# Last feed-forward of a four-layer model: who multiplies gate and lifted columns, and one step of lag

## The reference, cut to what matters

```python
def fake_quant_nvfp4(x, global_scale):
    xb = x.reshape(sh[:-1] + (sh[-1] // BLOCK, BLOCK))
    amax = jnp.max(jnp.abs(xb), axis=-1, keepdims=True)
    sc = jnp.clip(amax / FP4_MAX * global_scale, 0.0, FP8_MAX)
    sc8 = sc.astype(jnp.float8_e4m3fn).astype(jnp.float32)
    dq = sc8 / global_scale
    a = jnp.clip(jnp.abs(xb) / safe_dq, 0.0, FP4_MAX)
    q = jnp.sign(xb) * _FP4_VALS[jnp.digitize(a, _FP4_MIDS)]
    return (q * dq).reshape(sh)
gate_out = nvfp4_linear(x, gate_w, s_in[0])
up_out = nvfp4_linear(x, up_w, s_in[0])
hidden = jax.nn.silu(gate_out) * up_out
return nvfp4_linear(hidden, down_w, s_in_down[0])
```

## Time and profile before

| what | us |
|---|---|
| median of three runs | 1085.5 |
| lowest and highest of them | 1084.51, 1087.7 |
| span of the profiled execution | 1084.4 |
| DVE busy in the span | 885.9 |
| POOL busy in the span | 523.1 |
| ACT busy in the span | 686.2 |

### The profile page before, as it was taken

How to read it: one execution, slowest core, us unless ns; L and a number is a source line. 1 busy time by engine, 2 the same in 40 slices (tenths; PEclk the granted TensorE clock), 3 DMA queues, 4 the chain that set the end, 5 groups by cost and what they waited for, 6 DMA issues and landing times.

```text
span 1084.4 us, 30129 instructions
## 1 busy us (share of the span) xinstructions
PE 898.7 (83%) x11539; PEld 707.4 (65%) x11557; DVE 885.9 (82%) x2296; ACT 686.2 (63%) x1794; POOL 523.1 (48%) x612
## 2 busy tenths in 40 slices
PE   8999999999999932999689999978899999434443
PEld 5888889978887721566457778834478888222222
DVE  6999888878999961567568889889978888899997
ACT  6888864377776610444447777866678888555553
POOL 6444412254367676223287787255553332355554
PEclk9999999999999966899889999988899999655665
DMA  8760000000000012365111111000000000000000
GB/s 214 186 241 2 3 2 2 1 2 3 3 24 27 27 46 76 114 187 175 51 33 32 26 31 29 6 1 2 1 2 2 2 3 3 1 10 16 15 15 24
DMA packets 60526, 44.42 MB, mean 41 GB/s; under 512 B 15196, under 2 KB 55781, under 8 KB 59366
## 3 DMA queue, kind: packets, MB, share of 16 engines
q1 hardware_dynamic: 55718, 34.09, 10.6%
q0 software_dynamic: 4096, 8.34, 2.7%
q10 hardware_dynamic: 576, 0.13, 0.1%
HBM read 23.73 MB, written 18.87 MB: 39 GB/s over the span
## 4 chain that ended last, share of the span: by engine, by line
PE 63%; DVE 21%; issue 6%; POOL 5%; ACT 2%; DVEq 2%; DMA 1%; POOLq 0%; another core or an unknown queue 0%; SPq 0%; ACTq 0%
PE ps L747 10%; PE ps L706 9%; PE ps L674 7%; PE ps L586 4%; PE ps L720 4%; PE ps L692 4%; POOL q_out L1232 3%; DVE rowmax L1879 3%; PE ps L782 3%; PE ps L791 3%; PE ps L783 3%; PE ps L640 2%; PE ps L655 2%; PE ps L653 2%; DVE sm L1885 2%
## 5 line engine op out<-in xcount | busy, mean ns | idle before, releaser
L1879 DVE TENSOR_REDUCE rowmax<-ps 128x16 f32<-128x1024 f32 x128 | 155.8, 1217 | 35.7 <-PE ps L674 34.4
L1885 DVE TENSOR_TENSOR sm<-ps,rowmax 128x512 f32<-128x512 f32 x256 | 164.9, 686 | 3.4
L1038 ACT ACTIVATE pr<-ps 128x512 f32<-128x512 f32 x256 | 138.9, 595 | 38.2 <-PE ps L747 36.0
L747 PE MATMUL ps<-cst,sm 128*128 128x128 f32 x1024 | 138.9, 277 | 13.3 <-DVE sm L1885 12.2
L706 PE MATMUL ps<-vbd,pr 128*64 128x18 f32 x4096 | 140.3, 211 | 0.5 <-ACT pr L1038 0.5
L706 PEld LDWEIGHTS ps<-vbd,pr 128*64 128x64 f32 x4096 | 134.2, 138 | 1.4 <-ACT pr L1038 1.3
L1320 POOL TENSOR_SCALAR xn<-x_sb,mv_all,rstd_all 128x128 f32<-128x128 f32 x122 | 98.2, 805 | 71.7 <-PE ps L640 65.7
L747 PEld LDWEIGHTS ps<-cst,sm 128*128 128x128 f32 x1024 | 112.8, 141 | 26.3 <-issue 19.5
L938 ACT ACTIVATE qbd<-ps,bqp,cst 128x128 f32<-128x128 f32 x256 | 104.6, 463 | 6.2 <-PE ps L655 2.4
L975 ACT ACTIVATE vbd<-ps 64x128 f32<-64x128 f32 x256 | 70.8, 277 | 34.2 <-PE ps L692 26.6
L1202 POOL DMA_INDIRECT big<-expert_out,row_g x64 | 68.2, 1066 | 49.9 <-DMA expert_out<-xn_all 22.8
(11 more groups left out here) (299 smaller groups left out, 2348.3 us busy)
## 6 DMA issues: line engine op xcount, KB each, us to landing
slots<-hT SPq DMA_DIRECT2D x8, 1024.0 KB, 11.0
sm<-slots SPq DMA_DIRECT2D x32, 256.0 KB, 3.3
expert_out<-xn_all SPq DMA_DIRECT2D x16, 256.0 KB, 3.0
ew<-in_L_ffn_w SPq DMA_DIRECT2D x24, 128.0 KB, 2.6
out<-x_sb SPq DMA_DIRECT2D x32, 64.0 KB, 1.5
slots<-xn_all,row_s POOLq DMA_INDIRECT x64
big<-expert_out,row_g POOLq DMA_INDIRECT x64
x_sb<-in_x SPq DMA_DIRECT2D x1, 512.0 KB, 4.6
```

The costliest lines, as they stand in the source:

```text
L747: last = nc.tensor.transpose(turned[b][:, r * P:(r + 1) * P], sm[x][:, c:c + P], ident)
L1038: nc.scalar.activation(pr[y][:, b, :], turned[b], ACT.Exp, scale=SCALE).then_inc(p_ready[y], 1)
L1879: v.tensor_reduce(row3, sc, AX.X, ALU.max).then_inc(rowmax_ready[x], 1)
L1885: v.tensor_tensor(sm[x][:, :].rearrange("p (r g k) -> p r g k", r=RG, k=S)[:, part], sc[:, part], row3[:, part].unsqueeze(3).broadcast_to( ...
```

## The change: what it does

The multiplication of gate and lifted columns goes from DVE to POOL. ACT copies the lifted columns from PSUM to SBUF first (with the factor that L1725 applied), into `lifted_up`. Gates and copies are kept twice, for odd and even pairs, in `gate_both` and in parts of `xn_all`. Since POOL's product comes later in a step than DVE's did, the hidden values of a pair join the group four steps after its rows (GATED_LAG) and not three: groups 4 to 15 are full (12), 0 to 3 have rows only, 16 to 19 hidden values only, 20 in all.

```diff
@@ -41,6 +41,7 @@
 FP4_WEIGHT_STEPS, MEASURE_STEPS, ROUND_STEPS = 16, 7, 3
 BATCHES = ((0, 8), (8, 16), (16, 22), (22, 27), (27, 32))
 ROUTE = 6
+GATED_LAG = 4
 
 
 C_ID, C_TRI, C_ONE, C_DUP, C_CAUSAL = 0, 128, 256, 384, 512
@@ -143,8 +144,8 @@
     def fp4_order(eng, step, first):
 
 
-        for d in range(first, IT + 6):
-            step(d, *((d - lag if 0 <= d - lag < IT else None) for lag in (0, 2, 3, 5, 6)))
+        for d in range(first, IT + GATED_LAG + 3):
+            step(d, *((d - lag if 0 <= d - lag < IT else None) for lag in (0, 2, GATED_LAG, GATED_LAG + 2, GATED_LAG + 3)))
 
     def halves(x, h):
 
@@ -155,7 +156,7 @@
     def fp4_halves(g):
 
 
-        return halves(g if g < IT else None, g - 3 if g >= 3 else None)
+        return halves(g if g < IT else None, g - GATED_LAG if g >= GATED_LAG else None)
 
     def inverses_found(g):
 
@@ -265,13 +266,15 @@
         q_b = sb("q_b", [P, QW], BF16)
         rs_in = sb("rs_in", [P, T])
         mean_in = sb("mean_in", [P, T])
-        FP4_LAST = IT + 2
+        FP4_LAST = IT + GATED_LAG - 1
         fp4_in = [big[:, p * QW:(p + 1) * QW] for p in range(2)]
         fp4_r, fp4_m = [big[:, 2 * QW:3 * QW], q_r[:, 0:QW]], big[:, 3 * QW:4 * QW]
         fp4_b = [big[:, 4 * QW:4 * QW + QW // 2].bitcast(BF16), q_b]
         fp4_s = big[:, 5 * QW:5 * QW + 8 * (QW // Q16)].rearrange("p (n b) -> p n b", n=8)
         gs_w = sb("gs_w", [P, QMAX // Q16])
         hq = [q_out[:, XW + s * F2:XW + (s + 1) * F2] for s in range(NS)]
+        gates = [gate_both[:, :, :], xn_all[:, 0:NS * F2].rearrange("p (s n) -> p s n", s=NS)]
+        lifted_up = [xn_all[:, (1 + n) * NS * F2:(2 + n) * NS * F2].rearrange("p (s n) -> p s n", s=NS) for n in range(2)]
         hid_in = [q_in[:, XW + s * F2:XW + (s + 1) * F2] for s in range(NS)]
 
 
@@ -882,8 +885,7 @@
                 if px is not None:
                     for s in range(NS):
                         pe.wait_ge(xnT_ready[NS - 1], IT * FFN3 + px + 1)
-                        if h is not None:
-                            pe.wait_ge(hid_ready[NS - 1], IT + px)
+                        pe.wait_ge(gate_ready[0], IT + px)
                         for n in range(2):
                             last = nc.tensor.matmul(lifts[:, s, :] if n else bank(s, 1), xqT[s], wT[:, 2 + n, :], start=True, stop=True,
                                                     skip_group_check=True)
@@ -1011,9 +1013,12 @@
                     nc.scalar.activation(hid_in[s], bank(s, 1), ACT.Gelu).then_inc(hid_ready[s], 1)
 
             def gates3(px):
+                if px > 1:
+                    act.wait_ge(hid_ready[NS - 1], IT + px - 1)
                 for s in range(NS):
                     act.wait_ge(h_psum[s], IT + px + 1)
-                    nc.scalar.activation(gate[s][:, :], bank(s, 1), ACT.Silu, scale=unscale[:, 0:1]).then_inc(gate_ready[s], 1)
+                    nc.scalar.activation(gates[px % 2][:, s, :], bank(s, 1), ACT.Silu, scale=unscale[:, 0:1])
+                nc.scalar.activation(lifted_up[px % 2], lifts, ACT.Copy, scale=unscale[:, 1:2]).then_inc(gate_ready[0], 1)
 
             def attention(l):
                 k = ATTENTION_STAGE[l]
@@ -1259,8 +1264,8 @@
                                 ).then_inc(quotients[1], 1)
 
             def fp4_scaled(g):
-                if g > 3:
-                    pool.wait_ge(hqT_psum[NS - 1], IT + g - 3)
+                if g > GATED_LAG:
+                    pool.wait_ge(hqT_psum[NS - 1], IT + g - GATED_LAG)
                 elif g > 0:
                     pool.wait_ge(xnT_psum[NS - 1], IT * FFN3 + g)
                 low, high = fp4_halves(g)
@@ -1270,11 +1275,19 @@
                     over_blocks(q_out[:, part], fp4_b[last][:, part], fp4_s[:, 2 + g % 3, part.start // Q16:part.stop // Q16], Q16, ALU.mult
                                 ).then_inc(q_ready[1], 1)
 
+            def gated(px):
+                pool.wait_ge(quotients[1], 2 * (px + GATED_LAG - 1))
+                pool.wait_ge(gate_ready[0], IT + px + 1)
+                nc.gpsimd.tensor_tensor(fp4_in[(px + GATED_LAG) % 2][:, XW:QW].rearrange("p (s n) -> p s n", s=NS), lifted_up[px % 2],
+                                        gates[px % 2], ALU.mult).then_inc(hid_ready[NS - 1], 1)
+
             def ffn3(d, x, px, h, ph, done):
                 if 0 < d <= FP4_LAST:
                     fp4_quotients(d - 1)
                 if 2 < d <= FP4_LAST + 2:
                     fp4_scaled(d - 2)
+                if 0 <= d + 1 - GATED_LAG < IT:
+                    gated(d + 1 - GATED_LAG)
 
             def normal_rows(l, u):
                 xt = x_sb[:, u * D:(u + 1) * D]
@@ -1720,10 +1733,6 @@
                 top, magic, least = (fp4_ps[:, n, nb] if g >= 3 else fp4_s[:, 7, n * (XW // Q16):(n + 1) * (XW // Q16)] for n in range(3))
                 share, total, sc8, inv = (fp4_s[:, n, nb] for n in (0, 1, 2 + g % 3, 5 + g % 2))
                 if h is not None:
-                    for s in range(NS):
-                        dve.wait_ge(gate_ready[s], IT + h + 1)
-                    v.scalar_tensor_tensor(src[:, XW:QW].rearrange("p (s n) -> p s n", s=NS), lifts, unscale[:, 1:2], gate_both[:, :, :],
-                                           ALU.mult, ALU.mult).then_inc(hid_ready[NS - 1], 1)
                     dve.wait_ge(hid_ready[NS - 1], IT + h + 1)
                 if x is not None:
                     dve.wait_ge(xn_ready[NS - 1], IT * FFN3 + x + 1)
```

## The result

| | before | after |
|---|---|---|
| median of the runs, us | 1085.48 (4 runs, 1084.51 to 1087.70) | 1113.73 (4 runs, 1112.36 to 1114.58) |
| ratio | 1 | 1.0255, 95% interval 1.0241 to 1.0270 |
| span of the profiled execution, us | 1084.4 | 1112.1 |
| rounding of group 1 ends | 935.84 | 936.90 |
| from there to the end of the last residual | 145.58 | 172.23 |

The kernel became 2.55% slower. The stage that the change touches grew by 26.7 us, and another 1.1 us of the span came up ahead of it, where nothing was changed.

What follows compares the result with a forecast made beforehand. DVE sets the pace, and POOL's SBUF-reading product must take turns with DVE's rounding. Group 4 3.3 ahead, eleven steps of 10.7, last groups 27.35 and 8.13 put the end 28.0 later: 1113.5 us, range 1099 to 1119.

Steps and rivals of the forecast that it cites:

- groups 1 to 4, against before: Start of the stage: rounding of group 4 ends at 956.2 instead of 959.48, 3.3 us ahead of before.
- step of groups 5 to 15: Rounding to rounding in 11 groups: 10.7 us instead of 8.76, since POOL's product and DVE's rounding take turns; chance 0.66.
- first half, product's share, second half, rest: Behind the scaling: L1757's first half 0.70 us, POOL's product 2.26, second half 0.70, L1760 with L1761 2.05.
- groups 16, 17, 18: Last groups, hidden values only: 9.6, 9.15 and 8.6 us, together 27.35; group 18 has no product in front of it.
- last part: From the last group's rounding to the end of the last residual: 8.13 us, as before.
- The order that I let go first: After the scaling: DVE's waiting L1757 half first, then POOL's product, then the second half; other orders gave 10.8 or 10.5 us.
- The wait in the last group: Group 18: its division, with two SBUF inputs, waits 0.8 us for POOL's scaling.
- turns without loss: Rival: every start and gap of one engine is used by the other; step 9.7 to 9.8 us, total 1101.5; chance 0.12.
- the slower product: Rival: POOL's product takes 2.8 us instead of 2.40; step 11.1, total 1119; chance 0.08.
- rival of a free product: No turn taking between POOL's product and the rounding, DVE alone bounds: 7.45 us a step, total 1069; chance 0.09.
- The part of the prediction on L1725: L1725 leaving DVE does not give back its 1.31 us per step: L1757 must wait for POOL's scaling until T + 4.97.
- The copy on ACT: 1.11 us per copy of 1024 columns, cost 0 in steady steps; two copies come at the start, ending at 943.5.

Runs made afterwards that it cites:

- 4: Changed kernel with POOL's product placed between quotients and scaling instead of behind the scaling, nothing left out: ratio to the kernel before 1.0278, step 10.76 us.
- 9: Changed kernel without ACT's copy of the lifted columns, POOL multiplying whatever the buffer holds: 1.0224 of the kernel before, step 10.64 us.
- 1: Changed kernel with POOL's product replaced, from pair 2 on, by a memset about as long that reads nothing: 0.9961 of the kernel before, step 8.45 us.
- 2: Changed kernel with POOL's product left out from pair 2 on, a memset of 8 columns keeping the signal: 0.9957 of the kernel before, step 8.45 us.
- 3: Changed kernel with POOL multiplying only 512 of 1024 columns from pair 2 on: 1.0108 of the kernel before, step 9.53 us.
- 10: The changed kernel run once more, unaltered, on the chip of the run without ACT's copy: 1.0240 of the kernel before, step 10.64 us.
- 5: Changed kernel with the product back on DVE ahead of the measuring, both inputs from SBUF copies: 1.0099 of the kernel before, step 9.29 us.
- 6: Changed kernel with the product back on DVE behind the measuring, one input from PSUM, no ACT copy: 0.9996 of the kernel before, step 8.48 us.
- 8: Changed kernel with magnitudes of 512 of a full group's 1280 columns kept in PSUM: 1.0121 of the kernel before, step 9.67 us.
- the later sets: Experiments 5 to 8, then 9 and 10, each set with its own runs of the kernel before: 1069.76 us and 1071.28 us.
- experiment 7: The kernel before the change with ACT's gates moved ahead of its copies of transposed hidden values: 1.0007 of the kernel before, step 8.75 us.

## Why the prediction was right, step by step

| term of the prediction | predicted | measured | tested by |
|---|---|---|---|
| groups 1 to 4, against before | 3.3 less | 3.65 less | 4, 9 |
| step of groups 5 to 15 | 10.7 | 10.62 | 1, 2, 3 |
| of it: first half, product's share, second half, rest | 0.70, 2.26, 0.70, 2.05 | 0.68, 2.20, 0.68, 2.05 | |
| groups 16, 17, 18 | 9.6, 9.15, 8.6 | 9.56, 9.13, 8.57 | |
| last part | 8.13 | 8.15 | |
| last residual against before | 28.0 later | 27.7 later | 10 |
| time of the runs | 1113.5 | 1113.73 | |

The measured parts of the step are those of the timeline of 1009.99 to 1020.58, behind the scaling's end. The deciding step was to ask of each instruction of DVE and POOL whether they had ever overlapped, and what it had cost; three places elsewhere in the program had the answer, and experiments 1 to 3, 5, 6 and 8 confirm it from both sides. The order that I let go first (half, product, half) is the order of the trace. The wait in the last group is there as well: its division (L1749) took 1.59 for 0.69 in its first half, 0.90 where 0.8 was counted. Of the rivals, turns without loss (9.7 to 9.8 a step) fails on eleven steps of 10.59 to 10.66, and the slower product on 2.40 alone in experiment 4.

Three things were less good than the sum:

- The forecast of the whole was closer than its parts deserve, and that is luck. The stage grew by 26.7 us, not 28.0 (0.9 of the difference in the eleven steps, 0.35 in groups 1 to 4, 0.1 at the end); 1.1 us came from ahead of the stage. Experiments 1 to 4 have the changed kernel's code up to the stage and end the rounding of group 1 at 935.5 to 936.4, where the kernel before does so at 935.8 and the changed one at 936.9; in the later sets the changed kernel's second trace has 920.0, and experiment 7, with the code of before, 919.3. So 1.1 us is no more than executions differ by. Part of it may still belong to the changed program: from DVE's instruction at 760 us of the kernel before to that at 800, in the third layer's feed-forward and just behind it, the two traces with the code of before agree to 0.02 us and the other ten take 0.7 to 1.8 longer. TensorE's granted clock, as a mean over 780 to 790, is 0.95 of full speed before and 0.83 after. Whether that is chance stays open.
- The rival of a free product was priced at 1069 by a sum of DVE's work alone, 7.45 a step. Experiment 1 makes the product free of the turn taking, and the step is 8.45 (1082.76 against 1086.41 for the kernel before, 0.9961). The sum left out that the rounding must wait for POOL's quotients and scaling in any case, 4.98 + 3.46. The part of the prediction on L1725 had said just that; it was not carried over into the rival.
- The copy on ACT was counted with both its lengths at the start (2.2 us before group 4). The copy of pair 1 ended nearly as predicted (7.4 us behind the rounding of group 1, for 7.7), but without it groups 1 to 4 are only 1.02 shorter: POOL waited for the copies 0.2 and 0.6 us (L1281 in the groups above), and behind these waits its own queue of quotients and scalings ends last.

No kernel that does the whole computation was faster than the kernel before. Even a product that costs nothing gives 0.4%, and experiment 6, which leaves nothing out, cannot be told from the kernel before (0.9985 to 1.0006).

## What to carry to other kernels

Before work goes from DVE to an idle POOL, look at what POOL's idle time lies beside: here DVE ran two-input SBUF instructions there, the time was not free, and the moved work was added to the step almost in full (2.17 of 2.26 us). Look for a place in the trace where the two already overlap and compare the ends; busy shares hide it, since waiting is counted as busy. What moved such a limit here was an operand in PSUM, not another engine.

## What the runs showed of the hardware that was not expected

- A POOL instruction that only writes ran 2.37 us beside three DVE instructions with two SBUF inputs each (experiment 1) without lengthening any of them.
- The turn passes at once: the waiting half ended 0.68 behind the end of the scaling and of the product, and 640 columns at 1.1 ns are 0.70, where such a half takes 0.82 alone. So the rest of it lay under the other's work.
- The product of DVE from PSUM took 1.18 in experiment 6 behind the measuring and 1.28 ahead of it in the kernel before; why stays open: the shapes are the same, and in experiment 6 it took 1.18 with POOL's scaling beside it and with POOL idle.
